# Two float32-to-bfloat16 weight copies on GpSimd's DMA queue, cut into 16 slices of 256 rows

## The reference

```python
qkv = einsum('bsi,oi->bso', x, W_qkv); Q, K, V = split(qkv, 3)   # 16 heads of 64
Q, K = apply_rope(Q), apply_rope(K)
attn = softmax(where(causal, Q @ K.T / 8, -inf)) @ V
x = layernorm(x + einsum('bsi,oi->bso', attn, W_o))
x_dq = clip(round(x / scale), -127, 127) * scale
x = layernorm(x + einsum('bsi,oi->bso', x_dq, ternary - 1) + bias)
```

## Time and profile before

| | us |
|---|---|
| median of 2 runs (1660.31 to 1674.29) | 1667.3 |
| the execution that was profiled | 1663.35 |
| its span on the slowest core (core 1; the cores lie between 1643.6 and 1661.7) | 1661.7 |
| PE busy in the span | 1134.8 |
| ACT busy | 1003.8 |
| DVE busy | 562.6 |
| POOL busy | 34.7 |

### The profile page before, as it was taken

One profiled execution on the slowest core, in us unless ns is written; L12 is line 12 of the kernel. 1 busy time (PEld: TensorE's weight loads), 2 busy tenths in 40 slices (PEclk: granted clock), 3 DMA queues, 4 the chain that ended last, 5 costly groups with the idle time before them and its releaser, 6 DMA issues.

```text
span 1661.7 us, 18220 instructions; the slowest of 8 cores (1643.6 to 1661.7 us)
## 1 busy us (share of the span) xinstructions
PE 1134.8 (68%) x5064; PEld 384.4 (23%) x5064; DVE 562.6 (34%) x1147; ACT 1003.8 (60%) x1259; POOL 34.7 (2%) x59
## 2 busy tenths in 40 slices
PE   1000799999984466777778787888887875556563
PEld 0000444444441011111121121122112112222221
DVE  0000333323352455333323222211222225666664
ACT  0001455555553466888898888888888864445453
POOL 1000000000000000000000000000000000000000
PEclk9999999999997778999999899899999977878786
DMA  9999455766735423222432313222222010211111
GB/s 126 103 140 176 111 127 136 143 140 150 131 82 106 91 63 107 77 85 77 125 107 63 118 61 138 100 79 80 80 79 80 1 47 5 76 51 64 63 51 51
DMA packets 113009, 153.29 MB, mean 92 GB/s; under 512 B 38928, under 2 KB 93200, under 8 KB 108560
## 3 DMA queue, kind: packets, MB, share of 16 engines
q1 hardware_dynamic: 66688, 117.46, 22.3%
q0 software_dynamic: 12688, 26.29, 12.9%
q10 hardware_dynamic: 33536, 8.39, 3.1%
HBM read 132.26 MB, written 46.14 MB: 107 GB/s over the span
## 4 chain that ended last, share of the span: by engine, by line
PE 30%; ACT 21%; DMA 17%; DVE 12%; issue 11%; ACTq 5%; another core or an unknown queue 4%; DVEq 0%; SPq 0%; POOLq 0%
ACT exp_b L497 18%; DMA k_scr<-krot 11%; PE pAV L519 9%; DVE exp_b L508 6%; PE pSC L482 5%; PE pR L625 5%; PE pR L712 4%; PE pRaw L317 3%; DMA q_scr<-krot 2%; ACT recb L528 2%; PE pC L375 2%; DMA maskb<-masks 2%; ACTq L239 2%; ACTq L243 2%
## 5 line engine op out<-in xcount | busy, mean ns | idle before, releaser
L497 ACT ACTIVATE exp_b<-pSC 128x1024 bf16<-128x1024 f32 x640 | 606.9, 1046 | 148.7 <-PE pSC L487 136.3
L519 PE MATMUL pAV<-exp_b,v_run 128*128 128x512 bf16 x1280 | 417.5, 411 | 95.0 <-DVE exp_b L508 94.1
L508 DVE TENSOR_TENSOR exp_b<-exp_b,maskb 128x512 bf16<-128x512 bf16 x512 | 211.4, 425 | 374.3 <-ACT exp_b L497 311.5
L482 PE MATMUL pSC<-q_run,k_run 64*128 64x512 bf16 x640 | 255.0, 407 | 116.7 <-ACT exp_b L497 101.1
L487 PE MATMUL pSC<-q_run,k_run 64*128 64x512 bf16 x640 | 260.1, 415 | 0.0
L482 PEld LDWEIGHTS pSC<-q_run,k_run 64*128 64x128 bf16 x640 | 57.5, 94 | 415.7 <-issue 415.7
L519 PEld LDWEIGHTS pAV<-exp_b,v_run 128*128 128x128 bf16 x1280 | 77.5, 98 | 279.4 <-issue 279.4
L317 PE MATMUL pRaw<-x_T,w_kvT 128*128 128x512 bf16 x512 | 120.9, 382 | 1.3 <-ACT x_T L305 1.3
L323 ACT CAST kraw<-pRaw 128x512 bf16<-128x512 f32 x96 | 56.3, 586 | 98.6 <-PE pRaw L317 50.3
L375 PE MATMUL pC<-w_kvT,x_T 128*128 128x512 bf16 x512 | 115.7, 379 | 0.0
L271 PE MATMUL pD<-identb,w_st 128*128 128x128 bf16 x32 | 4.0, 307 | 150.5 <-DVE w_st L265 150.5
(11 more groups left out here) (95 smaller groups left out, 902.1 us busy)
## 6 DMA issues: line engine op xcount, KB each, us to landing
v_scr<-v_stg SPq DMA_DIRECT2D x32, 512.0 KB, 4.1
v_run<-v_scr SPq DMA_DIRECT2D x8, 2048.0 KB, 9.1
v_run<-v_scr SPq DMA_DIRECT2D x8, 1536.0 KB, 7.8
x_tm<-x_kv POOLq DMA_DIRECT2D x16, 512.0 KB, 8.4
k_scr<-krot SPq DMA_DIRECT2D x64, 128.0 KB, 2.9
v_run<-v_scr SPq DMA_DIRECT2D x8, 1024.0 KB, 5.4
k_run<-k_scr SPq DMA_DIRECT2D x8, 1024.0 KB, 6.7
xo<-x_own SPq DMA_DIRECT2D x16, 512.0 KB, 4.4
```

The lines of the kernel that those rows point to most:

```text
L482: s.add("T", (lambda sb_, bi, t: lambda te: te.matmul(pSC[sb_][:, 0:512], k_run[bi][0:64, t * 128:(t + 1) * 128], q_run[bi][0:64, :], star ...
L497: s.add("SC", (lambda eb, sb_: lambda sc: sc.activation(exp_b[eb][:, :], pSC[sb_][:, :], ACTF.Exp))(eb, sb_), reads=[f"pSC{sb_}"], writes= ...
L508: s.add("V", (lambda eb, moff, half: lambda v: v.tensor_tensor(exp_b[eb][:, half * 512:(half + 1) * 512], exp_b[eb][:, half * 512:(half + ...
L519: s.add("T", (lambda eb, bi, t, hh, n, pit: lambda te: te.matmul(pAV[pit][:, hh * 512:(hh + 1) * 512], v_run[bi][:, t * 256 + hh * 128: t ...
```

## The change

The one copy of wqkv becomes 12 DMAs of 256 rows each, and the one of wo_in becomes 4 of 256 rows. All 12 name the key wqkv_bf, all 4 the key wo_bf. What comes behind is unchanged, but its lines move down by 6: L239, L243, L247 become L245, L249, L253, and L288 becomes L294.

```diff
-            s.add("G", lambda g: g.dma_start(out=wqkv_bf, in_=wqkv), writes=["wqkv_bf"])
-            s.add("G", lambda g: g.dma_start(out=wo_bf, in_=wo_in), writes=["wo_bf"])
+            for rb in range(12):
+                s.add("G", (lambda rb: lambda g: g.dma_start(
+                    out=wqkv_bf[rb * 256:(rb + 1) * 256, :],
+                    in_=wqkv[rb * 256:(rb + 1) * 256, :]))(rb), writes=["wqkv_bf"])
+            for rb in range(4):
+                s.add("G", (lambda rb: lambda g: g.dma_start(
+                    out=wo_bf[rb * 256:(rb + 1) * 256, :],
+                    in_=wo_in[rb * 256:(rb + 1) * 256, :]))(rb), writes=["wo_bf"])
```

## The result

The changed kernel takes 1680.11 us in the median (1668.85 to 1740.12, 19 runs), the kernel before 1665.15 us (1655.03 to 1724.11, 18 runs) beside it. The ratio is 1.0084, 95% interval 1.0058 to 1.0110: 0.84% or some 14 us slower, clear of noise, and less than half of the 31 us that were forecast. The execution profiled took 1675.79 us with a span of 1674.2 us, on core 7.

The account below looks back on a forecast made before the run. Weight copies, then ScalarE's transposes and casts, bound the head before the first projection at 186.29 us. Sixteen slices of 7.2 us delay the third transpose 29.3 us; plus 2 gives +31.3, so 1694.7 or 1698.6, named 1697 us; range 1674 to 1716.

Parts of the forecast that it names:

- 31 us that were forecast: Shift of ScalarE's first cast and everything behind: third transpose 29.3 us later, plus 2 us, together +31.3 us.
- That the slices wait for one another, and that this is the cost: GpSimd's queue: slices sharing a key issue only after the previous landing, making 16 round trips in series.
- The path: Head of the program: ScalarE's queue ends later, delaying its first cast; from there to the end unchanged, 1504.5 us.
- The second transpose no longer stands: ScalarE's queue: the second transpose, whose issue stood 21.3 us, should run in the gaps between slices.
- the room of the x loads: GpSimd's x_tm and cs_b chain, queued behind the slices, has some 40 us of room before the first projections wait.
- I take 4.8 + 2.4 = 7.2 us: One slice on GpSimd's queue: 4.8 us moving, from the whole copy's rows, plus 2.4 us fixed, from the quiet x_tm pair.
- 120.0 had been forecast: ScalarE's third transpose: issued about 120.0 us, after the last landing at 118.96 and 1 us delay, instead of 90.68.
- +2 us on both: After the third transpose: an added x_tm half (3.4 us) against the first two transposes' rest, netted at +2 us.
- The first rival: Slices move faster if memory shared with a neighbour core sets 4.8 us: 5.83 us a slice, +9.4, 1676 us; chance 0.25.
- its two starting values: Bases for the shift: profiled 1663.35 us and median 1667.3 us, giving 1694.7 and 1698.6; 1697 us named between.
- The lower end of the range: Whole time: 1674 us, from a slice of 5.83 us and the lower base, with a little noise.
- The rival on the other side: Not slower: a lone slice reaches the queue's best rate, 4.8 us a slice, shift -7, 1660 us; chance 0.05.

Follow-up runs that it names:

- the comparison of two sizes: Waiting slices of 128 rows (24 + 8) against the changed kernel's 256 rows: 4.60 and 6.08 us from slice to slice; profiled executions 1725.7 and 1675.8 us.
- The last early start: Kernel before, reordered to copy and transpose keys and values first; query rows and wo follow in waiting 256-row slices, two in each of jobs 1 to 4: ratio 0.9818.
- the first early start: Kernel before, reordered: key and value rows copied and transposed first, query rows and wo copied behind the first x loads, ternary chain spread over jobs: ratio 1.0543.
- the second: The early order again, with ternary loads issued a job ahead, late copies behind the third x load, late transposes one by one: ratio 0.9992 to the kernel before.

## Why the prediction was wrong

**That the slices wait for one another, and that this is the cost: right.** The 14 waits stand in the trace, and without them the head of the program is where it was (first cast 152.8 us in the mean).

**The path: right.** Everything that the change costs is made before ScalarE's first cast (13.8 us in the mean of the cores, 14 us in the time), and the rest of the span is unchanged to 1.3 us. The second transpose no longer stands, the room of the x loads was not used up (GpSimd still waited 44.6 us for TensorE before its next x load; 50.7 us before).

**The step that failed: "I take 4.8 + 2.4 = 7.2 us" for a slice.** It measured 6.08 us, and both terms were off. The moving time was read from rows that follow one another while a neighbour core does the same (4.8 us); a row in a queue with gaps moves in 3.04 us by the DMA share and costs 3.0 us by the comparison of two sizes. I wrote that "nothing shows that it would fall": the 315 GB/s read and written by each core, and the different landings of cores 0 and 1, were hints that it might, and I used them for a rival only. The fixed part was read from a load into SBUF (2.4 us) and measures 3.0 to 3.1 us for a copy between HBM tensors. The errors were -1.8 and +0.6 us a slice. The 16 slices were put at 115.2 us and took 104.5; it would be 97 at 6.08 us each, but the first slice (9.9 us), the two at the end of wqkv_bf (13.6 us together) and some of the others took longer. So the third transpose went out at 108.33 us on this core and at 105.3 in the mean, where 120.0 had been forecast.

The Trainium skill, DMA: Bandwidth & Descriptors, section "Anatomy of one DMA — SWDGE (gpsimd) path", puts the constant of a DMA at about 2.0 us and names HBM as the heaviest target. The measurement of 3.0 to 3.1 us for HBM to HBM is above its number and in line with that remark.

**A smaller miss: "+2 us on both" after the third transpose.** On core 7 the 22 transposes and the loads beside them took 62.7 us from 108.33 to 171.04, and 63.0 us on the same core before (91.46 to 154.48); in the mean of the cores it was 62.6 and 63.1 us. The term was nothing. I had also carried core 1's 66.5 us to a run whose slowest core was another; on the same core the third transpose moved by 16.9 us (91.46 to 108.33).

**The first rival was the right one.** It names the shared memory, and with the measured 6.08 us its line gives 3.76 + 97.3 + 1 - 90.7 + 2 = +13.4 us, where 14 were measured. That close a match is partly luck: the line puts the third transpose at 102.1 us, where it went out at 105.3 in the mean, and adds the 2 us that were nothing. (The forecast adds its shift to 1665.3 us, the mean of its two starting values; by the same rule this rival comes to 1675 us and not 1676. The lower end of the range, 1663.35 + 9.4, comes to 1673 and not 1674.) What told the two apart beforehand is a question that the rows allowed: whether two numbers of a row's time, one taken under load by a neighbour and one without gaps, can be added to a fixed part that leaves gaps. They can't: the first contains the neighbour's share. The range, 1674 to 1716 us, held the time; the size of the slowdown was over twice too large. The rival on the other side fell because the best rate of the x_tm load, 2.4 us for 512 KB, is reached in a full queue of a lone core (2.46 us) but not by a lone row (3.04 us); with the fixed part at 3.0 us even that rate would have made 5.4 us, above the 5.2 us from which this rival decides.

## What to carry to other kernels

Where slices write one key, each waits for the one before, and the price of a slice is the fixed part of its round trip (here 3.1 us) unless another core fills the gap; at two rows for each DMA engine (1 MB written) the waits were free on eight cores, at one they cost 14 us in 16 slices; on a lone core the larger slices were not tried. A time read under contention is not the time of the same work with gaps in it: ask who shares the resource, and try one core alone. Slices with waits let what stands beside them through (the second transpose issued in 2.66 us in place of 21.3), which is worth their price only where that is urgent. The last early start has such slices beside its stores; how much of its gain is theirs and how much comes from their place no run separates.

## What the hardware showed that was not expected

- A core alone moved a row of the copy in 2.46 us, which is 64 KB read and 32 KB written by each of 16 DMA engines, or 425 GB/s read and 213 written, 638 in all. Where cores 0 and 1 ran, the same four rows of wo_bf took them 19.45 and 19.85 us, 4.9 and 5.0 us each, which makes 640 GB/s for both together: hardly more than one alone. The Trainium skill, DMA: Bandwidth & Descriptors, section "Specifications", gives 716 GB/s for the memory of two cores, and the runs stay 11% below it.
- The whole kernel, not the copy alone, is 3.9% faster on one core than on two (1592.0 and 1657.0 us, one run each, on two chips); on core 0, 48.5 us of the 65 are in the head (first cast at 104.45 and 152.97 us).
- A transposing DMA issued behind a large copy in GpSimd's software queue stands with it although its own queue is another: 21.3 us before, 12.1 us on the lone core, 44.8 us in the first early start, 41.7 us in the second. In the kernel before the issue ended at 90.59 us, as the x_tm load behind the copies landed (90.66), and on the lone core at 49.43 us (49.51). With the copy in waiting slices the same issue took 2.66 us, and with the same slices without waits 22.45 us.
